# Attention's output turned in 32x32 blocks by VectorE instead of by TensorE

## The reference

```python
q = _heads(x @ Wq + bq); k = _heads(x @ Wk + bk); v = _heads(x @ Wv + bv)
att = jnp.einsum('bhqd,bhkd->bhqk', q, k) * scale
att = jnp.where(causal[None, None], att, -jnp.inf)
y = jnp.einsum('bhqk,bhkd->bhqd', jax.nn.softmax(att, axis=-1), v)
qc = _heads(x @ Wcq + bcq); kc = _heads(cross_input @ Wck + bck); vc = _heads(cross_input @ Wcv + bcv)
attc = jnp.einsum('bhqd,bhkd->bhqk', qc, kc) * scale
y = y + jnp.einsum('bhqk,bhkd->bhqd', jax.nn.softmax(attc, axis=-1), vc)
y = y.transpose(0, 2, 1, 3).reshape(x.shape[0], T, C)
return y @ Wp + bp
```

## Time and profile before

| what | us |
|---|---|
| median of 3 runs | 1554.93 |
| lowest and highest run | 1553.13, 1565.95 |
| the profiled execution's own time | 1567.87 |
| its span, first to last instruction | 1565.1 |
| TensorE busy, share of the span | 1466.7, 94% |
| VectorE busy | 1124.9, 72% |
| ScalarE busy | 907.4, 58% |
| GpSimd busy | 548.4, 35% |

### The profile page before, as it was taken

The page is one execution under the profiler, slowest core; times in us unless marked ns, Lnnn a source line. Parts: engine busy times, 40 slices in busy tenths (PEclk is TensorE's granted clock), DMA queues, the critical chain, the costliest instruction groups (busy, mean ns, idle before and its releaser), DMA issues. The chain is left out here.

```text
span 1565.1 us, 26271 instructions
## 1 busy us (share of the span) xinstructions
PE 1466.7 (94%) x8868; PEld 717.5 (46%) x8868; DVE 1124.9 (72%) x3134; ACT 907.4 (58%) x1754; POOL 548.4 (35%) x1013
## 2 busy tenths in 40 slices
PE   8899999999999999999999999999998857999997
PEld 4443444444444444444453445344443323676674
DVE  7878887877888788778876887787785067455451
ACT  2177777677777777676777777767776500212211
POOL 4132333352344324332434333333213121443452
PEclk9599999999999999999999999999999877999999
DMA  6766483829374846575466738481900120444442
GB/s 189 121 142 84 89 111 103 118 66 147 101 106 85 144 103 103 98 157 82 91 116 125 100 81 127 106 117 63 138 4 3 42 86 14 117 99 123 119 99 50
DMA packets 82390, 155.25 MB, mean 99 GB/s; under 512 B 13008, under 2 KB 46416, under 8 KB 82256
## 3 DMA queue, kind: packets, MB, share of 16 engines
q1 hardware_dynamic: 74752, 142.43, 47.9%
q0 software_dynamic: 6144, 8.52, 3.2%
q10 hardware_dynamic: 1360, 2.62, 0.4%
HBM read 96.52 MB, written 53.08 MB: 96 GB/s over the span
## 5 line engine op out<-in xcount | busy, mean ns | idle before, releaser
L828 ACT ACTIVATE probs<-bank_ps 128x512 f32<-128x512 f32 (+1 forms) x1408 | 725.2, 579 | 236.7 <-PE bank_ps L610 229.9
L928 DVE TENSOR_REDUCE chunk_max<-bank_ps 128x1 f32<-128x512 f32 x1024 | 652.5, 684 | 125.2 <-PE bank_ps L649 122.4
L610 PE MATMUL bank_ps<-q_stack,k_stack 64*128 64x512 f32 (+3 forms) x1536 | 506.4, 422 | 41.2 <-ACT probs L828 37.3
L649 PE MATMUL bank_ps<-k_stack,q_stack 62*128 62x512 f32 (+3 forms) x1536 | 529.0, 432 | 7.0 <-DVE chunk_max L928 5.1
L649 PEld LDWEIGHTS bank_ps<-k_stack,q_stack 62*128 62x128 f32 x1536 | 248.8, 189 | 361.6 <-DVE chunk_max L928 211.5
L931 DVE CUSTOM_DVE_ANT_0 masked<-bank_ps,causal 128x128 bf16<-128x128 f32 (+3 forms) x512 | 233.4, 485 | 80.6 <-PE bank_ps L649 79.0
L610 PEld LDWEIGHTS bank_ps<-q_stack,k_stack 64*128 64x128 f32 x1536 | 235.1, 187 | 107.2 <-ACT probs L828 99.7
L1101 POOL TENSOR_TENSOR pool_idle<-pool_idle 128x1 f32<-128x1 f32 x292 | 57.0, 195 | 636.2 <-ACT probs L828 291.4
L628 PE MATMUL out_ps<-probs,v_cross 128*32 128x512 f32 x2048 | 277.1, 613 | 0.0
L1437 ACT ACTIVATE h<-h_ps,b1T 128x512 f32<-128x512 f32 x64 | 44.0, 687 | 227.3 <-PE h_ps L1369 227.3
L1369 PE MATMUL h_ps<-ff_yT,w1T 128*128 128x512 f32 x256 | 114.5, 601 | 0.6 <-DVE ff_yT L1450 0.6
(11 more groups left out here) (173 smaller groups left out, 1372.2 us busy)
## 6 DMA issues: line engine op xcount, KB each, us to landing
parts_dram<-parts SPq DMA_DIRECT2D x70, 512.0 KB, 2.7
k_stack<-parts_dram SPq DMA_DIRECT2D x180, 192.0 KB, 11.6
q_stack<-parts_dram SPq DMA_DIRECT2D x180, 128.0 KB, 10.6
w1T<-in_L_ffn_fc1s SPq DMA_DIRECT2D x8, 1024.0 KB, 5.7
w2T<-in_L_ffn_fc2s SPq DMA_DIRECT2D x8, 1024.0 KB, 7.4
z_rows<-z_sb SPq DMA_DIRECT2D x8, 528.0 KB, 13.9
x_sb<-in_x SPq DMA_DIRECT2D x8, 512.0 KB, 4.7
ctxT<-in_ctx SPq DMA_DIRECT2D x8, 512.0 KB, 11.6
```

Source lines behind the costliest of these rows:

```text
L610: mm = pe.matmul(bank_of(turn)[:, of.at:of.end], k_stack[base:base + SIDE, g, pair, of.keys:of.keys + P], q_stack[base:base + SIDE, g, pai ...
L649: return pe.matmul(bank[:, 0:n], q_stack[base:base + MAX_ROWS, g, pair, qc:qc + P], k_stack[base:base + MAX_ROWS, g, pair, k0:k0 + n], sta ...
L828: nc.scalar.activation(probs[:, buffer(u, i, p), side, columns], bank_of(("score", g, i, p, side))[:, columns], ACT.Exp, scale=SCALE)\
L928: nc.vector.tensor_reduce(dst, bank[:, 0:n], AX.X, ALU.max).then_inc(max_done, 1)
```

## The change

`u_sb` is turned by VectorE in blocks of 32x32, in place (`turn_heads`), so that within a block of 32 rows each head's four heads' rows become tokens: partition 32h + t holds token 32n + t of head h, column n holds block n. VectorE divides there (`divide`), GpSimd adds as before (`add_heads`), and when both units of a half of the batch are done, VectorE turns the half back with one more block transpose (`turn_back`) into yT, to which ScalarE adds the bias in place (`add_value_bias`). Since a block has 32 columns and a head 16, two units share a block: heads alternate between them (`head_in_half`), in v, in the fills and in `y_sb`. `OUTPUT_PLAN` says in which step each of these operations of VectorE stands. The pieces out_cross, out_self, yT0 and yT1 are gone, and `PLAN` has the others in new places. At the end of the last batch the same functions run one after the other, and eight products of ones keep TensorE going.

```diff
--- before.py
+++ after.py
@@ -32,6 +32,8 @@
 HALF_H = P // D
+UNITS_HALF = HALF_H // UH
+BLOCK = 32
 Q_PART = (0, 0, 1)
@@ -55,9 +57,8 @@
 V_PIECES = ("v", "vc0", "vc1")
-OUT_PIECES = ("out_cross", "out_self")
 PROJ_PIECES = ("proj0", "proj1")
-LATER = ("yT0", "yT1", *PROJ_PIECES, "zT0", "zT1", "gate")
+LATER = (*PROJ_PIECES, "zT0", "zT1", "gate")
 COL = {"q": (0, 512), "qc": (512, 1024), "k": (1024, 1536), "kc0": (1536, 2048), "kc1": (2048, 2560)}
@@ -68,14 +69,18 @@
-    (0, 2): (("vc0", 1),), (0, 3): (("out_cross", 0), ("out_self", 0)), (0, 4): (("v", 1),),
...
+    (0, 2): (("v", 1),), (0, 3): (("vc0", 1),), (0, 5): (("y0T0", 0), ("y0T1", 0)), (0, 6): (("vc1", 1),),
...
+OUTPUT_PLAN = {
+    (0, 1): ("turn_cross",), (0, 3): ("divide_cross", "turn_self"), (0, 5): ("divide_self",), (0, 8): ("turn_back",),
+    (1, 0): ("turn_cross",), (1, 2): ("divide_cross", "turn_self"), (1, 4): ("divide_self",), (2, 1): ("turn_cross",),
+    (2, 3): ("divide_cross", "turn_self"), (2, 4): ("divide_self",), (2, 5): ("turn_back",), (3, 1): ("turn_cross",),
+    (3, 2): ("divide_cross", "turn_self"), (3, 4): ("divide_self",),
 }
...
@@ -103,6 +106,11 @@
                          if name in HALF_PIECES and half == hf) for hf in range(2))
+def outputs_at(first, g, i):
+    return () if first and g == 0 else OUTPUT_PLAN.get((g, i), ())
@@ -124,14 +132,14 @@
-EPILOGUE = (("out_cross", 0), ("out_self", 0), ("yT0", 0), ("yT1", 0), ("proj0", 0), ("proj1", 0), ("zT0", 0),
-            ("zT1", 0), ("gate", 0))
-MEANWHILE = {"out_self": 1, "yT1": 1, "proj1": 4, "zT1": 1}
+EPILOGUE = (("proj0", 0), ("proj1", 0), ("zT0", 0), ("zT1", 0), ("gate", 0))
+BEFORE_LAST = 8
+MEANWHILE = {"proj1": 4, "zT1": 1}
-    return not (name in COL or name == "shift" or name in OUT_PIECES or name in PROJ_PIECES)
+    return not (name in COL or name == "shift" or name in PROJ_PIECES)
...
@@ -255,6 +263,11 @@
              for kind, chunk in (("cross", 0), ("cross", 1), ("self", 0)) for side in range(SIDES)]
+def head_in_half(slot, h):
+    return UNITS_HALF * h + slot % UNITS_HALF
@@ -300,9 +313,9 @@
         u_sb = sb("u_sb", [P, 2, T])
-        y_sb = sb("y_sb", [P, NT, C])
-        y_add = sb("y_add", [P, NT, UH, D])
-        rden = sb("rden", [P, 2, NT, UH])
+        y_sb = sb("y_sb", [P, KT, T // BLOCK, BLOCK])
+        y_add = sb("y_add", [P, T // BLOCK, D])
+        rden = sb("rden", [P, 2, T // BLOCK])
         yT = sb("yT", [P, KT, T])
...
@@ -464,10 +482,10 @@
                     sp.wait_ge(scores_ready, scores)
-                hf, at = slot // 2, slot % 2 * UH * D
+                hf = slot // UNITS_HALF
                 sp.wait_ge(parts_out, PARTS * (halves - 1))
-                heads = lambda part, a, e: parts_dram[hf, part, at:at + UH * D, a:e]\
-                    .rearrange("(h s d) n -> s d h n", s=SIDES, d=D)
+                heads = lambda part, a, e: parts_dram[hf, part, :, a:e]\
+                    .rearrange("(h s u d) n -> u s d h n", s=SIDES, u=UNITS_HALF, d=D)[slot % UNITS_HALF]
                 for r in range(len(Q_PART)):
...
@@ -625,7 +643,7 @@
                     for h in range(UH):
-                        mm = pe.matmul(out_ps[32 * h:32 * h + 32, of.q0:T], v[:, g // 2, of.tile, g % 2 * UH + h, :],
+                        mm = pe.matmul(out_ps[32 * h:32 * h + 32, of.q0:T], v[:, g // 2, of.tile, head_in_half(g, h), :],
                                        probs[:, buffer(u, i, h // 2), h % 2, of.at:of.end],
@@ -674,14 +692,8 @@
                                       row_max[:, unit % 2].rearrange("p h s t -> p (h s t)"), ident[:])
-                elif name in ("out_cross", "out_self"):
-                    s = int(name == "out_self")
-                    pe.wait_ge(u_ready, 2 * unit + s + 1)
-                    mm = transpose4(bank, [u_sb[:, s, t * P:(t + 1) * P] for t in range(NT)])
-                elif name in ("yT0", "yT1"):
-                    pe.wait_ge(y_done, UNITS * b + UNITS)
-                    mm = transpose4(bank, [y_sb[:, t, c * P:(c + 1) * P] for t in range(NT)])
                 elif name in ("proj0", "proj1"):
+                    pe.wait_ge(y_biased, KT * b + KT)
                     for t in (0, 1):
...
@@ -804,12 +814,11 @@
             pe.wait_ge(exp_done, N_EXP * UNITS * B)
+            multiply_ones(BEFORE_LAST)
             for n, (name, _) in enumerate(EPILOGUE):
                     pe.wait_ge(*freed(epilogue_piece(B - 1, n - SCORE_BANKS)))
-                if name == "proj0":
-                    pe.wait_ge(*freed(epilogue_piece(B - 1, EPILOGUE.index(("yT1", 0)))))
-                elif name == "gate":
+                if name == "gate":
                     pe.wait_ge(*freed(epilogue_piece(B - 1, EPILOGUE.index(("zT1", 0)))))
@@ -839,6 +848,12 @@
+            def add_value_bias(b, c):
+                act.wait_ge(turned_back, KT * b + c + 1)
+                nc.scalar.activation(yT[:, c, :], yT[:, c, :], ACT.Identity, bias=bias_v[:, 2, c:c + 1])\
+                    .then_inc(y_biased, 1)
             def piece(piece, bank):
...
@@ -879,6 +891,8 @@
                         exp_pair(b, g, i, 1)
+                        if "turn_back" in outputs_at(first, g, i):
+                            add_value_bias(b - (g == 0), int(g == 0))
                         if i == BEHIND - 1 and g > 0:
...
@@ -966,26 +981,44 @@
-                name, b, unit = piece.name, piece.of, piece.unit
+                name, b = piece.name, piece.of
                 dve.wait_ge(piece_full, piece.number + 1)
-                if name in OUT_PIECES:
-                    s = OUT_PIECES.index(name)
-                    g = unit % UNITS
-                    sums = bank[:].rearrange("p (t h d) -> p t h d", t=NT, h=UH)
-                    nc.vector.reciprocal(rden[:, s], sums[:, :, :, D]).then_inc(rden_done, 1)
-                    if s:
-                        dve.wait_ge(y_done, unit)
-                        y = y_add[:]
-                    else:
-                        y = y_sb[:, :, g * UH * D:(g + 1) * UH * D].rearrange("p t (h d) -> p t h d", h=UH)
-                    dve.wait_ge(rden_done, 2 * unit + s + 1)
-                    nc.vector.tensor_tensor(y, sums[:, :, :, 0:D], rden[:, s].unsqueeze(3).broadcast_to([P, NT, UH, D]),
-                                            ALU.mult).then_inc(y_part, 1)
+                c = PROJ_PIECES.index(name)
+                dve.wait_ge(xb_done, b + 1)
+                rows = x1[:, 2 * c:2 * c + 2, :].rearrange("p t c -> p (t c)")
+                nc.vector.tensor_tensor(rows, bank[:], rows, ALU.add).then_inc(proj_added, 1)
+            def turn_heads(unit, s):
+                dve.wait_ge(u_ready, 2 * unit + s + 1)
+                nc.vector.transpose(u_sb[:, s], u_sb[:, s]).then_inc(turned, 1)
+            def divide(unit, s):
+                sums = u_sb[:, s].rearrange("p (n c) -> p n c", c=BLOCK)
+                dve.wait_ge(turned, 2 * unit + s + 1)
+                nc.vector.reciprocal(rden[:, s], sums[:, :, D]).then_inc(rden_done, 1)
+                if s:
+                    dve.wait_ge(y_done, unit)
+                dve.wait_ge(rden_done, 2 * unit + s + 1)
+                nc.vector.tensor_tensor(y_add[:] if s else heads_of(unit), sums[:, :, 0:D],
+                                        rden[:, s].unsqueeze(2).broadcast_to([P, T // BLOCK, D]),
+                                        ALU.mult).then_inc(y_part, 1)
+            def turn_back(b, c):
+                dve.wait_ge(y_done, UNITS * b + UNITS_HALF * (c + 1))
+                nc.vector.transpose(yT[:, c], y_sb[:, c].rearrange("p n c -> p (n c)")).then_inc(turned_back, 1)
+            def output(b, g, name):
+                unit = UNITS * b + g - 1
+                if name == "turn_back":
+                    turn_back(b - (g == 0), int(g == 0))
+                elif name.startswith("turn"):
+                    turn_heads(unit, int(name == "turn_self"))
                 else:
-                    c = PROJ_PIECES.index(name)
-                    dve.wait_ge(xb_done, b + 1)
-                    rows = x1[:, 2 * c:2 * c + 2, :].rearrange("p t c -> p (t c)")
-                    nc.vector.tensor_tensor(rows, bank[:], rows, ALU.add).then_inc(proj_added, 1)
+                    divide(unit, int(name == "divide_self"))
@@ -1028,6 +1061,8 @@
                             if n == ahead_of_pieces(i):
+                                for name in outputs_at(first, g, i):
+                                    output(b, g, name)
                                 for at in pieces_at(first, last, g, i):
@@ -1078,6 +1113,12 @@
             batch(B - 1, False, True, False)
+            for s in range(2):
+                turn_heads(UNITS * B - 1, s)
+                divide(UNITS * B - 1, s)
+            dve.wait_ge(y_part, 2 * UNITS * B)
+            nc.vector.tensor_tensor(heads_of(UNITS * B - 1), heads_of(UNITS * B - 1), y_add[:], ALU.add).then_inc(y_done, 1)
+            turn_back(B - 1, 1)
```

(20 more changed lines are left out.)

21 lines of the change are left out of this document (10 added, 11 removed), and 9 rows, old and new, of the table PLAN.

## The result

The changed kernel takes 1595.69 us (median of 4 runs, 1592.22 to 1597.92), the one before in the same comparison 1558.09 (4 runs). The ratio is 1.0235, 95% interval 1.0184 to 1.0285: slower by 37.6 us, where 1553 was forecast with a range of 1534 to 1570. The profiled execution after took 1592.22 us, span 1590.5, 25.4 more than the span before. The profiled run of before was a long one (1567.87), hence the smaller difference there.

The account below looks back on a forecast made before the run. TensorE looked like the bound, limited by a step floor and a DMA chain. With the chain at 49 us, 5 x 0.6 - 4 - 1 = -2 gave 1553 us, its own range 1545 to 1563, 8 in 10 within 1534 to 1570.

Parts of the forecast that it names:

- Pieces, floor and price: TensorE's steps: ten pieces removed save 5.2 us, six more floor steps return 2.2, shift alone 1.0; net -2.0 per batch.
- +2.5: Thirty steps outside (3,8) to (0,10) gain 2.5 us; with the chain at 52.1, a batch becomes that much longer.
- VectorE: Ten block transposes of 128x512 per batch at 0.62 us add 6.2 us of VectorE work, priced at cost 0.
- The chain: DMA transfers from the shift store of (3,7) to unit 1's shift rows arriving: 52.1 us profiled, TensorE alone arriving after 50.9.
- I take 49: Chain length assumed for usual runs, between 46.4 and 50.9 us; a batch then costs +0.6.
- full borders: The five places between batches taken to carry the whole DMA chain; the first and last were called lighter.
- The last border: The last place between batches, lighter because no context is loaded, was to keep its gain of 2.0 us.
- second rival: Chain as slow as profiled, with waits of 5.7 us at (1,0) and clock drops: 1570, up to 1575; chance 0.12.
- +7.5: Sum over the program with the profiled 52.1 us chain: 5 x 2.5 - 4 - 1, giving 1575 in its own frame.
- The end: After the last batch, copy to yT was to take about 4 us instead of 5.1, a gain of 1.
- First rival: The chain is no limit, ending by 46.4 us; eight batches gain 2.0 each and the end 1: 1538; chance 0.28.
- Third rival: VectorE becomes the bound: transposes at 0.8 us, no slack at four unprotected steps, 22 us more, 1575; chance 0.08.

Follow-up runs that it names:

- the kernel before with shift first: The kernel before, with the context and the shift of slot 1 ahead of the fill of slot 3 on SP; 1556.34 us, ratio 0.9982.
- the two experiments: Source rows of the start's direct copies exchanged: the kernel before with those of after, 1562.11 us; the change, SP order also edited, with those of before, 1543.47 us.
- the edit on SP: Context and shift of slot 1 issued ahead of the fill of slot 3; 1551.77 us in the changed kernel, 1556.34 in the kernel before.
- the start's rows back: The changed kernel with context and shift ahead of slot 3's fill, its direct start copies reading the source rows of before; 1543.47 us, ratio 0.9895.
- the threefold turn: The changed kernel with context and shift ahead of slot 3's fill, each turn of u_sb done three times in place; 1575.30 us, ratio 1.0126.
- with gate back: The changed kernel with only gate and vc1 put back to (3,8), behind the shift of (3,7); 1574.12 us, ratio 1.0107.
- the change with shift first: The changed kernel with the context and the shift of slot 1 ahead of the fill of slot 3 on SP; 1551.77 us, ratio 0.9959.
- eight fillers: The changed kernel with eight products of ones on TensorE ahead of the shift wait at (1,0) of batches 2 to 7; 1595.76 us, ratio 1.0255.

## Why the prediction was wrong

Step by step, in the prediction's order.

*Pieces, floor and price.* Right. In the fourteen steps from (3,8) to (0,10) a clean batch fell from 49.6 to 45.1, -4.5 as worked out; the other steps gained 2.2 (+2.5 was expected). The net is -2.3 to -2.6 (-2.0 was taken; a clean batch of before is 147.00 or 146.75). A step without a piece still lasts 2.70, the unprotected (0,1) and (3,1) 2.49, shift alone 3.25.

*VectorE.* A turn is 702 ns, within the bounds of 485 and 798 but over the 0.62 taken; 7.0 us a batch instead of 6.2. Its cost of 0 held. The Trainium skill's figure ("VectorE: DVE Perf Modes", the three transpose paths, 311 ns for a 128x128 bf16 block) times four would have been 1.24 us, by the estimate made of it; the trace shows 0.70, so growth with the columns alone isn't what this shape shows.

*The chain.* Here the prediction failed, at "I take 49". The profile showed 52.1 us and the arithmetic from it was made: TensorE would come after 46.4, the wait grows by 4.5, a batch becomes 2.5 longer, 1575 in its own frame. TensorE did come after 46.2 at four of the five full borders. That arithmetic was then set aside since the median run was 13 us shorter than the profiled one, which I put down to a shorter chain in usual runs. It is not shorter in the change: 50.1 to 52.5 at the five full borders, and no trace of any run that waits at a full border has it under 50. The profiled run of before was long for other reasons too: of its 10.7 us over six batches of 147.00, some 4 are half clock behind (3,8), 5.7 lie at (1,0) and (1,1), and 1.2 are a wait for the context. Most borders of before showed no wait because TensorE came after 50.1 to 51.7 itself, as the trace of the kernel before with shift first shows, where nothing holds it; no trace shows the chain in a median run of before. A chain and an engine that arrive together look like no wait at all, and each us then taken from the engine is a us of wait.

*The last border* was to be lighter and keep its 2.0, for want of a context. It had 4.48 us of wait and a chain of 49.9. Only the first border was free.

*The clock.* The forecast priced a drop of the clock at nothing. The second rival had this mechanism, waits of 5.7 us with a drop once a batch, and got 0.12. Its 1570 to 1575 is still 21 to 26 short. A part of that is its frame: the +7.5 was worked out in the profiled run of 1567.87, where the sum would be 1583, but it was put on the median of 1554.93. Against batches of 147.00 the six are 28.8 us longer: 38.8 at (1,0) and (1,1) of five borders, less 2.6 in each of six batches (15.4), and 5.4 from elsewhere, nearly all of it clock drops behind the gate product at (3,6), in two of the six batches. The rival's price per border, 2.5 and 1.5, would be 4.0; the mean was 5.8 over 147.00. A full border's wait was 5.0 in the mean, and the base had no waits to take off: the +2.5 was worked out from a profiled batch that already had 1.15 us of it. And the clock fell for 6.8 to 10.2 us after the wait, which cost 2.6 a border and not 1.5. The added 3.6 at the start and 3.5 behind the last batch's start make the rest: 28.8 + 3.7 + 3.5 = 36.0 of 37.6.

*The start* was priced at nothing; the direct copies were not in the working. They cost 6 to 8 us in the medians of the two experiments, and 8 to 9 in their traces; the 3.6 above is what is left of it behind the shorter steps of the first batch.

*The end* was to gain 1. The data were ready 4.1 us behind the copy, as worked out, but the eight products of ones, which the diff shows, were not counted as work in front of the projection. It lost 1.7.

*First rival*, the chain is no limit: false for the change, but it is what the edit on SP makes true. It would then be 1538 by its arithmetic (8 x 2.0 + 1); 1551.77 was measured, and 1543.47 with the start's rows back. *Third rival*, VectorE: false, by waits that did not grow (3.6 us, weight loads 309.6) and by the threefold turn.

## What to carry to other kernels

When an engine arrives at a hand-over within a microsecond of a transfer chain, the absence of waits in a typical run says nothing of room: price every cut of the engine's work inside that stretch as a wait of the same length, and issue first the transfer that is waited for. Work that is only rearranged should be moved within one such stretch, or the stretch shortened first. And a changed layout has to be priced in every transfer that reads it, the ones of the start too.

## What the runs showed of the hardware

- A store of 32 KB alone lands in 1.5 us at the median; behind a fill and the context it was 12.4 to 15.3 us until SP could read it back (five full borders). Its place in the queue, not its size, was worth 44 us in the program.
- TensorE's clock fell to half for 6.8 to 10.2 us behind each of the six waits of 3.3 to 6.3 us, and with gate back behind waits of 2.2 to 3.7 us too; behind the one of 1.70 it stayed at full speed. With four products of ones ahead of the wait it fell behind waits of 2.33 (twice) and 3.54, and not behind those of 0.40, 1.35 and 2.05. Eight products in place of the wait kept it up.
- With the load gone the clock fell in another place. In the change with shift first it is at half in the last four steps of the last batch; in the control it isn't. Busy time from 1210 to 1230 us, change with shift first, then before with shift first:

```profile
1210.00:1230.00 20.00, 18.81 (x75) 7.42 (x74) 1.68 (x5) 9.43 (x20) 2.41 (x10) 0.55 0.25 80
```

```profile
1210.00:1230.00 20.00, 18.13 (x111) 8.14 (x111) 0.95 (x4) 13.04 (x27) 2.92 (x9) 1.00 0.16 54
```

  These four steps are 6.4 us longer than in the change with eight fillers, most of the 7.3 by which the end is longer. The missing pieces don't explain it: with eight fillers, and with gate back, the same pieces are gone and the last 20 us of attention have the full clock (1.00), while the trace of before, with all pieces, has the drop too (0.81 from 1225 to 1245 us). What sets it off, and the single drops behind (3,6) and (3,8) in some batches, stays open.
- A copy from 16 partitions to others took longer when the sources were every second block of 16: the median from issue to landing rose from 2.8 to 3.8 us for `k_stack` in the change and in the kernel before with its source rows, and fell back to 2.8 in the change with the rows of before.
- A block transpose of 128x512 in f32 on VectorE took 702 to 711 ns, in place or not, about as long as the maximum of the same shape (683).
